# Attention schedule: extra products at other steps, small products behind the scores, statistics ahead of the maximum, a stage one step later

## The chip, the cores and the metric

One core of a Trainium2 chip runs the whole program in one launch. The metric is the device time in microseconds of one execution. The engines are TensorE (PE; PEld is its weight load), VectorE (DVE), ScalarE (ACT), GpSimd (POOL) and SyncE (SP), which issues most DMAs. Each takes its instructions in order, and they signal each other by semaphores.

## The reference, cut to what matters

The model adds to x, one after the other: a gated feed-forward net, a state space block, the feed-forward net again, a mixture of experts, an attention, and the mixture again. Only the attention is touched. It has 2 sequences of 1024 tokens and 16 heads of 64, so 32 heads of 1024 x 1024 scores:

```python
dots = jnp.einsum('bhid,bhjd->bhij', q, k) * SCALE
m = jax.nn.softmax(dots, axis=-1)
diag = jnp.diagonal(m, axis1=-2, axis2=-1)
mu = diag.mean(axis=-1, keepdims=True)
sd = diag.std(axis=-1, ddof=1, keepdims=True)
keep = jnp.abs((diag - mu) / sd) <= Z_THRESH
valid = keep[..., :, None] & keep[..., None, :]
masked = jnp.where(valid, dots, NEG)
attn = jax.nn.softmax(masked, axis=-1)
...
out = jnp.einsum('bhij,bhjd->bhid', attn, v)
```

A head thus needs its whole score matrix once for the softmax's diagonal, then a mask out of the diagonal's statistics, the largest unmasked score of each row, and the scores again for the masked softmax.

## The kernel before

**Steps.** The attention is a software pipeline. A head's rows are cut into 8 blocks of 128 (`BLK`), and one step t handles one block of each stage. `due(t, offset, n)` (L1576) gives the head h and block k for which t = offset + 8h + k, with k < n. So an offset modulo 8 is the place of a stage in the period of eight steps in which each head goes through. The offsets stand at L1572 and L1573. Every engine has its own loop over t (`attention_pe`, `_act`, `_dve`, `_pool`, `_sp`) and in it a fixed order of `if`s, which is the order of its queue.

**Stages of a head.** QK projection (one step, `AT_QK`): ScalarE rounds it to a high part (`round_qk`, L2142), VectorE forms the low part (`rest_of_qk`, L2237), and SyncE copies both with the halves of the partitions swapped into `at_kq` (`move_parts`, four DMAs, L1805 and L1806). Scores (8 steps, L1957 and L1958): VectorE takes the diagonal (L2253), ScalarE the exponential with its sum (L2157). Statistics: reciprocals (`first_stats`), the mean by a small product (L1965, `negate_mean` reads it), deviations on ScalarE, the sum of squares by a second small product, `keeps` (L2287 to L2295, ending in `at_dropped`), and the mask turned into a row by a third (L1972, `mask_rows`), which SyncE spreads through DRAM. Best (8 steps, L1997 and L1998): scores again in high parts, masked and reduced to `at_row_max` by VectorE (L2262). A fourth small product turns the maxima (L1972, `shift_rows`), and two DMAs bring them to `at_shift_row`. Turned scores (8 steps, L2007 and L2008, and the shift product at L1878, with `at_shift_row` as an operand): ScalarE's exponential (`at_e`, L2165), VectorE's cast to a high part (L2382), GpSimd's subtraction for the low part (L2409). Two steps later `weigh` multiplies by the values (L1878 into `at_pv_ps`). ScalarE copies the sum of a head (L2204); the denominators go by DMA to VectorE (L2343, L2345), back through DRAM and spread (L1838), and GpSimd normalizes (L2421). For every second head there is an output projection, and VectorE adds it to x (L2364). Values are projected in two parts for every four heads (`group_due`, L1927).

**PSUM.** All these products but `weigh` share three tiles, `at_ps0` to `at_ps2`, in turn. `attention_slots` (L1604) lists the slots in order: in each step turned scores, scores, a slot that a small product and the best product of the step share (the small one first, in its corners), and then an extra one (QK, values or output) where one is due. `slot_free` (L1640) makes a product wait for the reader of the slot three before it:

```python
    kind, h, k = m.slot_order[n - 3][-1]
```

and a best product also for the reader of the small one in its slot.

**Order on TensorE within a step** (L2087 on): turned scores, small product, scores, weighing, best product, extra, weighing, extra. Where weighing and best are both due, products run as pairs on the upper and lower half of the rows, and the extra is in two halves around the second weighing.

**Before and behind.** A normalization of x stands ahead of the first step; the last head has its own end without DMAs (`last_norm`, L2315).

Of the kernel before, what the change touches and what calls it, by code (L numbers as in the profile page):

```python
# [9 lines left out]
ALU = mybir.AluOpType  # L10
# [10 lines left out]
BIG = 2.0 ** 100  # L21
# [23 lines left out]
BLK = SEQ // P  # L45
NH = BATCH * HEADS
# [1513 lines left out]

AT_FIRST, AT_LAST = -BLK * 2, BLK * (NH - 1) + BLK * 5 + 1
STATS, DEVS = 8, 5
HI, LO = 0, 1
TOP, LOW = slice(0, HD), slice(HD, P)
# [2 lines left out]
PARTS = 4  # L1569


AT_SPLIT, AT_QK, AT_SCORES, AT_STATS, AT_MEAN, AT_SQUARE, AT_MASK, AT_BEST, AT_SHIFT = -11, -8, 0, 8, 9, 10, 11, 13, 21  # L1572
AT_TURNED, AT_PV, AT_PV_OUT, AT_RECIP, AT_SPREAD, AT_NORM, AT_OUT = 22, 24, 32, 34, 35, 37, 39  # L1573


def due(t, offset, n=1):  # L1576
# [12 lines left out]


def pair_due(t):
    at = due(t, AT_OUT)
    return at[0] if at and at[0] % 2 == 1 else None


def small_due(t):
# [262 lines left out]
def attention_pe(c, m):  # L1859
# [227 lines left out]
    for t in range(AT_FIRST, AT_LAST):  # L2087
        weighed, tested = due(t, AT_PV, BLK), due(t, AT_BEST, BLK)
        apart = bool(weighed and tested)
        if at := due(t, AT_TURNED, BLK):  # L2090
            turned_scores(*at)
        if at := due(t, AT_MEAN):
            mean(at[0])
        if at := due(t, AT_SQUARE):
# [2 lines left out]
            turn_mask(at[0])  # L2097
        if at := due(t, AT_SHIFT):
            turn_shift(at[0])
        if at := due(t, AT_SCORES, BLK):  # L2100
            scores(*at)
        if apart:
            weigh(*weighed, False)
        if tested:
# [119 lines left out]
def attention_dve(c, m):  # L2224
# [107 lines left out]
    for t in range(AT_FIRST, AT_LAST):  # L2332
# [3 lines left out]
                attention_later_norm_dve(c, m)  # L2336
        if at := group_due(t - 1):
            rest_of_values(*at)
        if (at := due(t, AT_RECIP)) and at[0] == LAST:
            last_norm()  # L2340
        elif at:
            dve.wait_ge(sem["den_move"], 16 * (at[0] + 1))
            dve.eng.tensor_scalar(m.den[:], m.den[:], 1.0 / BIG, None, ALU.max).then_inc(sem["at_recip"])  # L2343
            dve.wait_ge(sem["at_recip"], 2 * at[0] + 1)
            dve.eng.reciprocal(m.recip[:], m.den[:]).then_inc(sem["at_recip"])  # L2345
        if (h := pair_due(t - 1)) is not None:
            pair, b = h % HEADS // 2, h // HEADS
            cols = slice(b * SEQ, (b + 1) * SEQ)
            dve.wait_ge(sem["at_out"], h // 2 + 1)
            dve.wait_ge(sem["attn_load"], 2 * 16)  # L2350
            dve.wait_ge(sem["attn_out_load"], 16)
            if h == LAST:
                for hf in range(2):
                    cols = slice(b * SEQ + hf * CH, b * SEQ + (hf + 1) * CH)
                    dve.wait_ge(sem["at_out"], h // 2 + hf + 1)
                    dve.wait_ge(sem["x_attn"], h // 2)
                    dve.eng.tensor_tensor(c.x[:, cols], c.x[:, cols], slot("out", h)[:, HALF[hf]],
                                          ALU.add).then_inc(sem["x_attn"])
            elif pair == 0:
                dve.eng.scalar_tensor_tensor(c.x[:, cols], slot("out", h)[:], c.b_out[:, 0:1], c.x[:, cols],  # L2360
                                             ALU.add, ALU.add).then_inc(sem["x_attn"])
            else:
                dve.wait_ge(sem["x_attn"], h // 2)
                dve.eng.tensor_tensor(c.x[:, cols], c.x[:, cols], slot("out", h)[:], ALU.add).then_inc(sem["x_attn"])  # L2364
        if at := due(t, AT_MEAN):
            negate_mean(at[0])
        if at := due(t, AT_SQUARE):
            negate_square(at[0])
        if at := due(t, AT_MASK):
            mask_rows(at[0])  # L2370
        if at := due(t, AT_SHIFT):
            shift_rows(at[0])
        if at := due(t, AT_SCORES, BLK):
            diagonal(*at)
        if at := due(t, AT_STATS):
            first_stats(at[0])
        if at := due(t, AT_TURNED, BLK):
            e = at[0] * BLK + at[1]
            dve.wait_ge(sem["at_exp"], e + 1)
# [2 lines left out]
            dve.eng.tensor_copy(m.e_hi[e % 3][:], m.e[e % 2][:]).then_inc(sem["at_hi"])  # L2382
        if at := due(t, AT_BEST, BLK):
            best(*at)
        if at := due(t, AT_SQUARE):
            keeps(at[0])
    dve.wait_ge(sem["x_attn"], ATTN_SUMS)


# [269 lines left out]
```

## Time and profile before

| | |
|---|---|
| median of 3 runs | 1979.87 us (1979.25 to 1979.98) |
| the profiled execution | 1980.71 us, span from first to last instruction 1979.4 us, clock 0.987 |
| PE busy | 1786.4 us, 90% |
| DVE busy | 1404.6 us, 71% |
| POOL busy | 1193.8 us, 60% |
| ACT busy | 1159.7 us, 59% |
| at_e_lo, POOL L2409 | 613.1 us, 256 times 2395 ns |
| maximum, DVE L2262 | 314.1 us, 256 times 1227 ns |
| cast at_e_hi, DVE L2382 | 247.8 us, 256 times 968 ns |

Busy times of engines run beside each other. A matmul's record overlaps the next one's, so lengths of steps are read from starts of the same kind of product, not from sums of durations. "[idle before <-releaser]" on a row is the time for which the engine did nothing ahead of it, and what ended that. The attention runs from about 712 us to 1854 us of the span.

### The profile page before, as it was taken

The page shows a single profiled execution, that of the slowest core. Times are in us where ns is not written, and L with a number is a line of the kernel's source. Part 1 is how long each engine was busy: PE and PEld are TensorE (multiplying, and loading weights), DVE is VectorE, ACT ScalarE, POOL GpSimd, SP SyncE. Part 2 cuts the span into 40 slices and gives each one's busy share as a digit, 9 for nine tenths or more (in the row PEclk, how much of TensorE's full clock was granted, in tenths as well). Part 3 has the DMA queues.
Part 4 walks back from the last instruction along what each step waited for, and adds up shares of the span by engine and source line. Part 5 has one row for each costly group of instructions (what it writes and reads, how often), then busy time and mean ns, then how long its engine had stood idle before and what let it go on. Part 6 is the DMA issues. An engine that isn't in the chain of part 4 may idle for free. (4 is left out here: it accounts for less than half of the span.)

```text
span 1979.4 us, 29905 instructions
## 1 busy us (share of the span) xinstructions
PE 1786.4 (90%) x11064; PEld 1213.2 (61%) x11064; DVE 1404.6 (71%) x2493; ACT 1159.7 (59%) x1715; POOL 1193.8 (60%) x660
## 2 busy tenths in 40 slices
PE   9998999789998986899989899898989898988888
PEld 5873444336875654666666667666666676665466
DVE  5617899986427754677777777777777777787676
ACT  5326777745326456666666666666666666663544
POOL 5542767963535430576666767676767666667454
PEclk9998999999999997999999999999999999999999
DMA  2000000000000013212122121212121212100100
GB/s 96 1 0 0 0 0 0 0 1 0 1 20 29 1 51 75 52 45 58 45 48 55 38 64 35 68 35 58 45 57 46 57 45 56 44 12 17 53 6 16
DMA packets 43665, 66.03 MB, mean 33 GB/s; under 512 B 24769, under 2 KB 26177, under 8 KB 43265
## 3 DMA queue, kind: packets, MB, share of 16 engines
q1 hardware_dynamic: 43056, 63.54, 12.4%
q8 instruction: 88, 1.44, 0.3%
q10 hardware_dynamic: 432, 0.59, 0.1%
q14 instruction: 57, 0.46, 0.1%
q0 software_dynamic: 32, 0.00, 0.0%
HBM read 29.05 MB, written 1.24 MB: 15 GB/s over the span
## 5 line engine op out<-in xcount | busy, mean ns | idle before, releaser
L2409 POOL TENSOR_TENSOR at_e_lo<-at_e,at_e_hi 128x1024 fp32r<-128x1024 f32 x256 | 613.1, 2395 | 353.9 <-DVE at_e_hi L2382 348.4
L2165 ACT ACTIVATE at_e<-at_ps,at_dropped 128x1024 f32<-128x1024 f32 x256 | 285.7, 1116 | 199.7 <-PE at_ps L1878 189.3
L2157 ACT ACTIVATE at_ps<-at_ps,at_neg_diag 128x1024 f32<-128x1024 f32 x256 | 278.6, 1089 | 138.3 <-DVE at_neg_diag L2253 137.0
L2262 DVE CUSTOM_DVE_ANT_0 at_ps<-at_ps,at_mask 128x1024 f32<-128x1024 f32 x256 | 314.1, 1227 | 3.0 <-PE at_ps L1998 1.3
L2382 DVE CAST at_e_hi<-at_e 128x1024 fp32r<-128x1024 f32 x256 | 247.8, 968 | 31.8 <-ACT at_e L2165 30.1
L1957 PE MATMUL at_ps<-at_kq,at_qk 64*128 64x512 f32 x768 | 235.3, 414 | 6.9 <-DVE at_row_max L2262 4.5
L1958 PE MATMUL at_ps<-at_qk,at_kq 64*128 64x512 f32 x768 | 235.7, 414 | 0.0
L2007 PE MATMUL at_ps<-at_qk,at_kq 64*128 64x512 f32 x768 | 224.4, 398 | 1.6 <-DVE at_row_max L2262 1.2
L2008 PE MATMUL at_ps<-at_kq,at_qk 64*128 64x512 f32 x768 | 224.6, 399 | 0.0
L1878 PE MATMUL at_pv_ps<-at_e_hi,at_v_hi 64*128 64x512 f32 x980 | 218.0, 436 | 0.0
L1056 POOL TENSOR_TENSOR mb_work<-mb_work,mb_c 128x1024 f32<-128x1024 f32 x64 | 151.6, 2370 | 97.7 <-DVE mb_work L1025 97.6
L421 POOL TENSOR_TENSOR ffn_lo<-ffn_hid,ffn_hi 128x512 fp32r<-128x512 f32 x96 | 127.2, 1328 | 132.1 <-DVE ffn_hi L338 132.1
L1878 PE MATMUL at_pv_ps<-at_e_hi,at_v_lo 64*64 64x512 f32 x980 | 195.3, 390 | 0.0
L1878 PE MATMUL at_pv_ps<-at_e_lo,at_v_hi 64*128 64x512 f32 x980 | 194.6, 389 | 0.0
L2253 DVE CUSTOM_DVE_ANT_0 at_junk_diag<-at_ps,ident 128x128 bf16<-128x128 f32 x256 | 74.0, 290 | 154.9 <-PE at_ps L1958 154.2
L2007 PEld LDWEIGHTS at_ps<-at_qk,at_kq 64*128 64x128 f32 x768 | 139.8, 185 | 34.4 <-DVE at_row_max L2262 4.2
L1957 PEld LDWEIGHTS at_ps<-at_kq,at_qk 64*128 64x128 f32 x768 | 134.2, 190 | 34.3 <-issue 10.2
L1025 DVE TENSOR_TENSOR_SCAN mb_work<-mb_work,mb_u_ps 128x1024 f32<-128x1024 f32 x64 | 146.3, 2286 | 6.4 <-PE mb_y_ps L652 1.2
L1500 POOL TENSOR_TENSOR moe_hid_lo<-moe_prod,moe_hid_hi 128x512 fp32r<-128x512 f32 (+1 forms) x72 | 92.8, 1290 | 95.6 <-ACT moe_hid_hi L1332 95.6
L338 DVE CAST ffn_hi<-ffn_hid 128x512 fp32r<-128x512 f32 x96 | 64.0, 671 | 120.8 <-ACT ffn_hid L309 119.5
L2008 PEld LDWEIGHTS at_ps<-at_kq,at_qk 64*128 64x128 f32 x768 | 139.8, 185 | 6.3 <-issue 4.2
L652 PE MATMUL mb_y_ps<-mb_work,ident 128*128 128x512 f32 x256 | 132.1, 602 | 8.4 <-DVE mb_dtx L949 6.8
(392 smaller groups left out, 4243.1 us busy)
## 6 DMA issues: line engine op xcount, KB each, us to landing
at_kq<-at_qk SPq DMA_DIRECT2D x128, 256.0 KB, 4.2
at_mask<-at_mask_dram SPq DMA_DIRECT2D x32, 256.0 KB, 3.6
at_recips<-at_recip_row SPq DMA_DIRECT2D x31, 256.0 KB, 4.4
ffn_h_raw<-in_h SPq DMA_DIRECT2D x2, 1024.0 KB, 8.0
at_head_w_raw<-in_w_qkv SPq DMA_DIRECT2D x32, 64.0 KB, 3.9
x<-in_x SPq DMA_DIRECT2D x4, 256.0 KB, 5.0
moe_gate_in<-in_gate_in SPq DMA_DIRECT2D x2, 512.0 KB, 4.0
moe_up_in<-in_up_in SPq DMA_DIRECT2D x2, 512.0 KB, 4.3
```

What stands on the lines that cost most here:

```text
L1025: dve.eng.tensor_tensor_scan(m.state[i % MB_STATES_HELD], m.d_a[i % MB_DECAYS], m.u_ps[:], 0.0, ALU.mult, ALU.add).then_inc(sem["mb_scan"])
L1056: pool.eng.tensor_tensor(m.state[i % MB_STATES_HELD], m.state[i % MB_STATES_HELD], m.c_sb[i % 3], ALU.mult).then_inc(sem["mb_hc"])
L1878: mm = pe.eng.matmul(bank, w[rows], moving[rows], start=first, stop=last)
L1957: pe.eng.matmul(ps[:, HALF[0]], own[TOP, q, rows], swapped[TOP, k, HALF[0]], start=(n == 0), stop=(n == 2))
L1958: mm = pe.eng.matmul(ps[:, HALF[1]], swapped[LOW, q, rows], own[LOW, k, HALF[1]], start=(n == 0), stop=(n == 2))
L2007: pe.eng.matmul(ps[:, HALF[0]], swapped[TOP, k, keys], own[TOP, q, HALF[0]], start=(n == 0), stop=False)
L2008: pe.eng.matmul(ps[:, HALF[1]], own[LOW, k, keys], swapped[LOW, q, HALF[1]], start=(n == 0), stop=False)
L2157: act.eng.activation(ps[:], ps[:], ACT.Exp, scale=SCALE, bias=m.small["neg_diag"][s][:, blk:blk + 1], accum_out=m.small["sums"][s][:, blk: ...
L2165: act.eng.activation(m.e[e % 2][:], slot("turned_scores", h, blk)[:], ACT.Exp, scale=SCALE, bias=m.small["dropped"][h % SLOTS][:, blk:blk ...
L2262: dve.eng.tensor_tensor_reduce(out=ps[:], in0=ps[:], in1=m.mask[h % 2][:], scale=1.0, scalar=-BIG, op0=ALU.add, op1=ALU.max, accum_out=m.s ...
L2382: dve.eng.tensor_copy(m.e_hi[e % 3][:], m.e[e % 2][:]).then_inc(sem["at_hi"])
L2409: pool.eng.tensor_tensor(m.e_lo[e % 3][:], m.e[e % 2][:], m.e_hi[e % 3][:].bitcast(F32), ALU.subtract).then_inc(sem["at_lo"])
```

## The change

The offsets move: the head weights' split from -11 to -6, QK from -8 to -3; turned scores from 22 to 23, and all that follows them by one step (weighing, its copy, reciprocal, spread, normalization); the output projection from 39 to 43, for the last head 40. Values follow the weighing (`group_due`), so they move by one step too. On TensorE the scores go ahead of the small products. On VectorE the diagonal and `first_stats` go ahead of the small products' readers, `keeps` ahead of the cast and the maximum, and the denominator's two operations behind the small readers. No instruction is added or removed but for the loops' one more step.

```diff
--- before.py
+++ after.py
@@ -1560,7 +1560,7 @@
 
 
 
-AT_FIRST, AT_LAST = -BLK * 2, BLK * (NH - 1) + BLK * 5 + 1
+AT_FIRST, AT_LAST = -BLK * 2, BLK * (NH - 1) + BLK * 5 + 2
 STATS, DEVS = 8, 5
 HI, LO = 0, 1
 TOP, LOW = slice(0, HD), slice(HD, P)
@@ -1569,8 +1569,8 @@
 PARTS = 4
 
 
-AT_SPLIT, AT_QK, AT_SCORES, AT_STATS, AT_MEAN, AT_SQUARE, AT_MASK, AT_BEST, AT_SHIFT = -11, -8, 0, 8, 9, 10, 11, 13, 21
-AT_TURNED, AT_PV, AT_PV_OUT, AT_RECIP, AT_SPREAD, AT_NORM, AT_OUT = 22, 24, 32, 34, 35, 37, 39
+AT_SPLIT, AT_QK, AT_SCORES, AT_STATS, AT_MEAN, AT_SQUARE, AT_MASK, AT_BEST, AT_SHIFT = -6, -3, 0, 8, 9, 10, 11, 13, 21
+AT_TURNED, AT_PV, AT_PV_OUT, AT_RECIP, AT_SPREAD, AT_NORM, AT_OUT, AT_LAST_OUT = 23, 25, 33, 35, 36, 38, 43, 40
 
 
 def due(t, offset, n=1):
@@ -1589,8 +1589,10 @@
 
 
 def pair_due(t):
+    if t == LAST * BLK + AT_LAST_OUT:
+        return LAST
     at = due(t, AT_OUT)
-    return at[0] if at and at[0] % 2 == 1 else None
+    return at[0] if at and at[0] % 2 == 1 and at[0] != LAST else None
 
 
 def small_due(t):
@@ -2089,6 +2091,8 @@
         apart = bool(weighed and tested)
         if at := due(t, AT_TURNED, BLK):
             turned_scores(*at)
+        if at := due(t, AT_SCORES, BLK):
+            scores(*at)
         if at := due(t, AT_MEAN):
             mean(at[0])
         if at := due(t, AT_SQUARE):
@@ -2097,8 +2101,6 @@
             turn_mask(at[0])
         if at := due(t, AT_SHIFT):
             turn_shift(at[0])
-        if at := due(t, AT_SCORES, BLK):
-            scores(*at)
         if apart:
             weigh(*weighed, False)
         if tested:
@@ -2336,13 +2338,6 @@
                 attention_later_norm_dve(c, m)
         if at := group_due(t - 1):
             rest_of_values(*at)
-        if (at := due(t, AT_RECIP)) and at[0] == LAST:
-            last_norm()
-        elif at:
-            dve.wait_ge(sem["den_move"], 16 * (at[0] + 1))
-            dve.eng.tensor_scalar(m.den[:], m.den[:], 1.0 / BIG, None, ALU.max).then_inc(sem["at_recip"])
-            dve.wait_ge(sem["at_recip"], 2 * at[0] + 1)
-            dve.eng.reciprocal(m.recip[:], m.den[:]).then_inc(sem["at_recip"])
         if (h := pair_due(t - 1)) is not None:
             pair, b = h % HEADS // 2, h // HEADS
             cols = slice(b * SEQ, (b + 1) * SEQ)
@@ -2362,18 +2357,26 @@
             else:
                 dve.wait_ge(sem["x_attn"], h // 2)
                 dve.eng.tensor_tensor(c.x[:, cols], c.x[:, cols], slot("out", h)[:], ALU.add).then_inc(sem["x_attn"])
+        if at := due(t, AT_SCORES, BLK):
+            diagonal(*at)
+        if at := due(t, AT_STATS):
+            first_stats(at[0])
         if at := due(t, AT_MEAN):
             negate_mean(at[0])
         if at := due(t, AT_SQUARE):
             negate_square(at[0])
+            keeps(at[0])
         if at := due(t, AT_MASK):
             mask_rows(at[0])
         if at := due(t, AT_SHIFT):
             shift_rows(at[0])
-        if at := due(t, AT_SCORES, BLK):
-            diagonal(*at)
-        if at := due(t, AT_STATS):
-            first_stats(at[0])
+        if (at := due(t, AT_RECIP)) and at[0] == LAST:
+            last_norm()
+        elif at:
+            dve.wait_ge(sem["den_move"], 16 * (at[0] + 1))
+            dve.eng.tensor_scalar(m.den[:], m.den[:], 1.0 / BIG, None, ALU.max).then_inc(sem["at_recip"])
+            dve.wait_ge(sem["at_recip"], 2 * at[0] + 1)
+            dve.eng.reciprocal(m.recip[:], m.den[:]).then_inc(sem["at_recip"])
         if at := due(t, AT_TURNED, BLK):
             e = at[0] * BLK + at[1]
             dve.wait_ge(sem["at_exp"], e + 1)
@@ -2382,8 +2385,6 @@
             dve.eng.tensor_copy(m.e_hi[e % 3][:], m.e[e % 2][:]).then_inc(sem["at_hi"])
         if at := due(t, AT_BEST, BLK):
             best(*at)
-        if at := due(t, AT_SQUARE):
-            keeps(at[0])
     dve.wait_ge(sem["x_attn"], ATTN_SUMS)
 
 
```

## Rows read from the trace of the kernel before

**Rows 1.** PE, PEld, DVE, ACT, POOL: busy us (instructions); clock, DMA share, GB/s

```profile
795.00:1735.00 940.00, 852.92 (x7270) 624.70 (x7266) 703.34 (x1510) 609.57 (x910) 640.81 (x305) 1.00 0.20 50
```

**Rows 2.** Waits of PE: line, what ended them, total us, times, longest

```profile
PE at_ps L1965 <- DVE at_qk L2237: 43.7, 28, 1.6
PE at_ps L1972 <- DVE at_dropped L2295: 26.3, 23, 2.1
```

**Rows 3.** Timeline, PE (start us, us): marks opening steps 2, 3, 4, 6, 0, 1, 2

```profile
973.65 0.40 PE L1878 MATMUL at_ps<-at_shift_row,at_minus 64*128 64x512 f32 x2
...
977.20 0.39 PE L1878 MATMUL at_ps<-at_shift_row,at_minus 64*128 64x512 f32 x2
...
981.88 0.39 PE L1878 MATMUL at_ps<-at_shift_row,at_minus 64*128 64x512 f32 x2
...
988.63 0.39 PE L1878 MATMUL at_ps<-at_shift_row,at_minus 64*128 64x512 f32 x2
...
995.23 0.39 PE L1878 MATMUL at_ps<-at_shift_row,at_minus 64*128 64x512 f32 x2
...
1000.61 0.39 PE L1878 MATMUL at_ps<-at_shift_row,at_minus 64*128 64x512 f32 x2
...
1005.89 0.39 PE L1878 MATMUL at_ps<-at_shift_row,at_minus 64*128 64x512 f32 x2
```

**Rows 4.** Timeline, PE: marks around values and QK; around an output projection

```profile
1054.97 0.39 PE L1878 MATMUL at_ps<-at_shift_row,at_minus 64*128 64x512 f32 x2
...
1059.62 0.40 PE L1878 MATMUL at_ps<-at_shift_row,at_minus 64*128 64x512 f32 x2
...
1063.19 0.39 PE L1878 MATMUL at_ps<-at_shift_row,at_minus 64*128 64x512 f32 x2
...
1067.77 0.41 PE L1878 MATMUL at_ps<-at_shift_row,at_minus 64*128 64x512 f32 x2
...
1227.59 0.41 PE L1878 MATMUL at_ps<-at_shift_row,at_minus 64*128 64x512 f32 x2
...
1232.54 0.41 PE L1878 MATMUL at_ps<-at_shift_row,at_minus 64*128 64x512 f32 x2
```

**Rows 5.** Timeline, PE: the mean's product of heads 8 and 24

```profile
1002.57 0.27 PE L1965 MATMUL at_ps<-at_row_sum_parts,at_ones 64*128 64x2 f32 x2 [1.57 <-DVE at_qk L2237]
...
1540.93 0.27 PE L1965 MATMUL at_ps<-at_row_sum_parts,at_ones 64*128 64x2 f32 x2 [1.56 <-DVE at_qk L2237]
```

**Rows 6.** Timeline, DVE: casts, a maximum, the low part of QK

```profile
990.21 0.69 DVE L2382 CAST at_e_hi<-at_e 128x1024 fp32r<-128x1024 f32 x1 [0.16 <-ACT at_e L2165]
...
993.52 2.75 DVE L2382 CAST at_e_hi<-at_e 128x1024 fp32r<-128x1024 f32 x1 [0.17 <-ACT at_e L2165]
...
996.20 1.22 DVE L2262 CUSTOM_DVE_ANT_0 at_ps<-at_ps,at_mask 128x1024 f32<-128x1024 f32 x1
...
1001.20 1.23 DVE L2237 TENSOR_TENSOR at_qk<-at_ps,at_qk 128x1024 fp32r<-128x1024 f32 x1 [0.72 <-ACT at_qk L2142]
...
1061.54 1.08 DVE L2382 CAST at_e_hi<-at_e 128x1024 fp32r<-128x1024 f32 x1
```

**Rows 7.** Timeline, POOL: low parts and a normalization

```profile
987.73 2.40 POOL L2409 TENSOR_TENSOR at_e_lo<-at_e,at_e_hi 128x1024 fp32r<-128x1024 f32 x1
...
990.26 2.90 POOL L2421 TENSOR_TENSOR at_heads_out<-at_pv_sb,at_recips 64x1024 f32<-64x1024 f32 x1
...
993.33 2.40 POOL L2409 TENSOR_TENSOR at_e_lo<-at_e,at_e_hi 128x1024 fp32r<-128x1024 f32 x1 [0.17 <-POOL at_heads_out L2421]
...
996.35 2.38 POOL L2409 TENSOR_TENSOR at_e_lo<-at_e,at_e_hi 128x1024 fp32r<-128x1024 f32 x1 [0.63 <-DVE at_e_hi L2382]
```

**Rows 8.** One tile's instructions, ns min/median/max, first and last start

```profile
L2292 DVE TENSOR_SCALAR at_keep<-at_dev,at_limit,at_varies x32: 290/1033/1072, 758.0 to 1779.4; 128x8 f32<-128x8 f32 x32
```

**Rows 9.** SyncE's last of four part transfers, and L1806's times to landing

```profile
1003.07 1.03 SPq L1806 DMA_DIRECT2D at_kq<-at_qk  x1
...
DMA to landing us min/median/max: 3.8/4.5/6.0
```

## The prediction

> **What bounds the kernel now.** I read three views in turn. First, the busy time of each engine in the steady stretch of the attention: TensorE is busy 852.92 of 940 us at a granted clock of 1.00, and VectorE, GpSimd and ScalarE 703, 641 and 610 us [rows 1]. So TensorE's work sets the pace, and about 9% of it is waiting. Second, TensorE's waits: the product for the mean (L1965) waits 28 times for VectorE to read the QK projection (L2237), 43.7 us, and the turned mask (L1972) waits 23 times for `at_dropped`, 26.3 us [rows 2]. Third, the timeline, with the shift product (L1878 on `at_shift_row`) as the mark that occurs once a step. The difference of two marks is the length of a step, and that, not the idle time shown, is the price of a wait: after a wait the pipeline also has to fill again.
>
> The marks give a price list. Two steps without an extra or a small product take 6.60 us (988.63 to 995.23) [rows 3], so one takes 3.30. The step with the square takes 3.55 and the one with the turned shift 6.75 - 3.30 = 3.45, so a small product that waits for nothing costs 0.25 or 0.15 [rows 3]. The mask's step takes 4.68, 1.23 over its unstalled 3.45. The mean's step takes 5.28, 1.73 over the square's. A QK projection that waits for nothing takes its step to 4.58, so costs 1.28 [rows 4]; in the head of rows 3 that step took 5.38, 0.80 more. A values product costs 4.65 - 3.30 = 1.35, and the step after it, which waits for its reader, takes 3.57, 0.27 over [rows 4]. An output projection costs 4.95 - 3.30 = 1.65 [rows 4].
>
> Per head the work alone comes to 8 x 3.30 + 1.28 (QK) + 0.80 (four small products) + 0.68 (two values parts in four heads) + 0.83 (one output in two heads) = 29.99 us. Sixteen heads took 538.36 us, 33.65 each [rows 5]. So **3.66 us per head are waits**.
>
> **The change part by part.** A step's products go turned scores, small, scores, weighing, best, extra; after the change the small one comes behind the scores. An extra takes one of three PSUM tiles in turn, so what stands three slots behind it needs its reader. In the kernel before, that is the small product in the next step where there is one, and TensorE is held with scores, weighing and best queued behind it. By residue of the step in its head of eight, small products stand at 1, 2, 3 and 5 in both kernels. Extras move from QK at 0, values at 6 and 2, output at 7 to QK at 5, values at 7 and 3, output at 3; each is then followed by 6, 0 or 4, where nothing small stands.
>
> 1. *Mean.* 1.73 us per head goes. QK's reader is now due only at the best product of step 6. It ends 1.82 us behind the mark (1001.20 + 1.23 - 1000.61), and the product waiting for it began at 1.96 [rows 3, 6, 5]. The same arrangement exists already behind the values at step 6, and cost 0.27 [rows 4]. I take 0.27 back; bounds 0 and 0.4.
>
> 2. *Mask.* `keeps` runs ahead of the high-part cast and the maximum, and the mask's product behind the scores, so `at_dropped` is there more than a microsecond early, and the values' reader is gone from this step. 1.23 us goes. In exchange four tiny VectorE operations, and the two of the denominator, stand ahead of the cast. `at_keep` takes 0.29 us when nothing is in its way and 1.03 at the median [rows 8]: the difference is waiting for GpSimd. Ahead of the cast the sum is some 0.8 us on VectorE; the product that would wait for it (the mask, then the best) has about that much room. On TensorE I take 0, bounds 0 and 0.4 per head.
>
> 3. *QK at 0.* Its step holds 0.80 us of waiting in the head of rows 3, which is the late maximum behind the slow cast of point 5, and less where an output or values step goes before. It goes from here, and comes back as point 5.
>
> 4. *QK's parts by DMA.* The projection is now three steps ahead of its scores instead of eight. The last of the four transfers is issued 2.46 us behind the mark (1003.07 - 1000.61) and lands 4.5 us later at the median, 6.0 at most [rows 3, 9]: 6.96 to 8.46. Two steps are then 3.57 + 3.30 = 6.87, and the scores stand 0.23 behind that mark (estimate), at 7.1. So TensorE may wait 0 to 1.4 us. Taken at 0, because point 5's wait comes later in the same stretch and covers it. Uncovered, it costs up to 1.4 per head.
>
> 5. *GpSimd's normalization.* It moves from step 5 to 6, behind the subtraction `at_e_lo`, and the head weights' split from 5 to 2. I follow it from step 6's mark (0). The cast behind a PSUM reader starts at 1.92 (1061.54 - 1059.62) and takes 0.69 alone [rows 4, 6]. `at_e_lo` follows at 2.69 for 2.40, the normalization 0.13 behind it at 5.22 [rows 7]. The next cast stands 1.58 behind its mark (990.21 - 988.63), at 3.57 + 1.58 = 5.15: just ahead. The normalization takes 2.90, to 8.12, the next `at_e_lo` starts at 8.29 (gap 0.17) and ends at 10.69 [rows 7]. The cast of step 0 is due at 6.87 + 1.58 = 8.45, so it is late by 0.16 and is held, as the one at 993.52 is, which took 2.75 us and was 0.54 behind GpSimd's end [rows 6, 7]. The maximum then ends 1.69 behind GpSimd's end, at 12.38 [rows 6, 7]. In the kernel before such a delay met the QK step's best product. Now the mean at step 1 needs that PSUM tile: it would be ready 0.92 behind its mark (estimate), 6.87 + 3.30 + 0.92 = 11.1, and waits until about 12.5. **1.4 us come back** in the three heads of four that have no values product at step 7 (that one gives 1.35 of room): 1.05 per head.
>
> The Trainium skill, page "SBUF — State Buffer", section "SBUF: two separate sides", says that VectorE's fast modes and GpSimd share a port pair by an exclusive lock, held for a whole instruction. By that rule the cast at 993.52 is held by `at_e_lo`, and the trace agrees: 2.75 us for work of 0.69. The rule speaks against moving `keeps` ahead of the cast.
>
> 6. *Values and output.* Their readers are waited for at steps 4 and 0 by the best product: 0.27 twice in four heads, 0.14 per head. The output's reader (one addition) has the room. The work itself is unchanged.
>
> Sum per head: -3.66 + 0.27 + 1.05 + 0.14 = -2.20 us, a period of about 31.45. Over the 28 heads in which everything runs, -61.6. Everything after the scores is **one step later**, so the drain has one more step, bound by the loop cast, subtraction, cast: 3.02 us from start to start [rows 7]: +3.0. The filling stretch has the QK parts due after three short steps, but smaller waits for statistics; I take 0, bounds -4 and +6. The total is -58.6. The profiled execution took 1980.71 us for a span of 1979.4; that is 0.8 us over the median of 1979.87, so the sum goes on the median: **1921 us**.
>
> **The rivals.** (a) *The normalization costs nothing.* If the cast of step 0 comes 0.16 us earlier or `at_e_lo` later, point 5 vanishes: 1921 - 28 x 1.05 = 1892 us. For it: a margin smaller than the jitter of a DMA. Against it: the casts and GpSimd repeat to 0.1 us, and in the kernel before the same race is lost by 0.19 (993.33 against 993.52) [rows 6, 7]. (b) *The queue of VectorE and GpSimd binds more.* After the held cast the two recover only 3.30 - 3.02 = 0.28 us a step [rows 3, 7], and `keeps`, the split at step 2 and the denominator's operations eat that. If the mask's and the shift's products then also wait, with the QK parts uncovered, 0.4 to 1.0 us per head come on top: 1932 to 1949, middle 1941. (c) *Slower than before: QK's parts.* SyncE is one queue; the parts stand behind the spread of the reciprocals (step 4, which waits for a write that itself waits for VectorE's step 3) and the shift (step 5). Up to 1.4 us past the scores' time is covered; from there each microsecond is 28 us. It decides above 1.4 + 2.1 = 3.5 us past, a landing 8.1 us after the last issue instead of 4.5 to 6.0 [rows 9]; at 9.1 the time is about 2007. Nothing in rows 9 comes near. (d) *The change doesn't do what it says:* the small products still share a slot with the best product and wait for the maximum before it for as long as they waited for QK. Then nothing moves but the drain: 1980 to 1983. The room of 0.7 us in an undisturbed step speaks against it.
>
> If the lock goes to the normalization in the tie at 5.15 against 5.22, the held cast is step 7's, and the waits are about 0.9 at step 0's best product and 0.4 at the mean: 1.3 in place of 1.4, the same forecast. The skill's rule (the first to start gets the port pair) would give the time of my forecast.
>
> **How the numbers follow.** Forecast 55%, range 1908 to 1934 by the bounds of points 1, 2 and the filling; (a) 20%; (b) 19%; (c) 3%; (d) 3%. The range reaches to (a) and the end of (b): 1890 to 1950. Within 0.2% (4 us) is what a measurement can't tell from no change. Faster 0.94, same 0.03, slower 0.03.
>
> **What would show it.** After: TensorE's wait for L2237 at the mean gone, and a small one at the best product (L1997-L1998) in its place; the wait for `at_dropped` gone; the step with QK 4.75 (1.28 + 3.45) long; the mean's step either 3.55, which is (a), or near 4.9 with a wait for `at_row_max`, which is the forecast; scores waiting for `at_kq` by DMA at most 1.4 us. I am wrong if TensorE still waits more than 2.5 us per head, or if the marks of plain steps move from 3.30.

## The result and the profile after

The changed kernel takes **1923.93 us** (median, 1923.52 to 1926.94) against 1979.92 in the same comparison: a ratio of 0.9726, 95% interval 0.9714 to 0.9737. 1921 was forecast. The profiled execution took 1923.52 us for a span of 1922.0 us.

First TensorE's busy time and its waits. Ahead of the windows row stand the columns of [rows 1]; the waits are ordered as in [rows 2]. Lines have shifted by two: L1967 is the mean's product, L1959 and L1960 are the scores, L1880 takes the place of L1878.

```profile
795.00:1675.00 880.00, 854.66 (x7234) 631.25 (x7232) 650.25 (x1508) 596.71 (x908) 629.32 (x306) 1.00 0.22 54
```

```profile
PE at_ps L1967 <- DVE at_row_max L2264: 16.2, 18, 1.2
...
PE at_ps L1959 <- DMA at_kq<-at_qk: 14.2, 10, 6.4
```

TensorE is busy 97% of the stretch, where it was 91% [rows 1]. Both waits of [rows 2] are gone: nothing at the mean waits for QK's reader, nothing at the mask for `at_dropped`. Two new ones stand in their place, and both were named ahead: the mean's product waits for the maximum, and the first scores of a head wait for the QK parts by DMA. The second line is mostly the filling stretch: three of its ten waits are there, with 10.3 of the 14.2 us.

The marks of a head without values or output, on the timeline of TensorE. They open steps 5, 6, 7, 0, 1, 2 and 3:

```profile
968.40 0.39 PE L1880 MATMUL at_ps<-at_shift_row,at_minus 64*128 64x512 f32 x2
...
973.16 0.39 PE L1880 MATMUL at_ps<-at_shift_row,at_minus 64*128 64x512 f32 x2
...
976.74 0.40 PE L1880 MATMUL at_ps<-at_shift_row,at_minus 64*128 64x512 f32 x2
...
980.04 0.39 PE L1880 MATMUL at_ps<-at_shift_row,at_minus 64*128 64x512 f32 x2
...
983.83 0.39 PE L1880 MATMUL at_ps<-at_shift_row,at_minus 64*128 64x512 f32 x2
...
988.35 0.40 PE L1880 MATMUL at_ps<-at_shift_row,at_minus 64*128 64x512 f32 x2
...
991.77 0.40 PE L1880 MATMUL at_ps<-at_shift_row,at_minus 64*128 64x512 f32 x2
```

Steps 5, 6, 7, 0, 1 and 2 take 4.76, 3.58, 3.30, 3.79, 4.52 and 3.42 us. Set beside [rows 3], a plain step is still 3.30; QK's step is 4.76 where it was 5.38; the mean's is 4.52 where it was 5.28, for another reason. Two rows of the mean's product, 16 heads apart as in [rows 5], give 506.58 / 16 = 31.66 us a head instead of 33.65:

```profile
985.72 0.27 PE L1967 MATMUL at_ps<-at_row_sum_parts,at_ones 64*128 64x2 f32 x2 [0.82 <-DVE at_row_max L2264]
...
1492.30 0.27 PE L1967 MATMUL at_ps<-at_row_sum_parts,at_ones 64*128 64x2 f32 x2 [1.03 <-DVE at_row_max L2264]
```

Where the mean's wait comes from is on the timelines of GpSimd and VectorE in the same head, the counterparts of [rows 6] and [rows 7]:

```profile
978.38 2.87 POOL L2422 TENSOR_TENSOR at_heads_out<-at_pv_sb,at_recips 64x1024 f32<-64x1024 f32 x1
981.42 2.40 POOL L2410 TENSOR_TENSOR at_e_lo<-at_e,at_e_hi 128x1024 fp32r<-128x1024 f32 x1 [0.17 <-POOL at_heads_out L2422]
```

```profile
978.33 0.70 DVE L2385 CAST at_e_hi<-at_e 128x1024 fp32r<-128x1024 f32 x1 [0.17 <-ACT at_e L2167]
...
982.16 2.21 DVE L2385 CAST at_e_hi<-at_e 128x1024 fp32r<-128x1024 f32 x1
984.30 1.22 DVE L2264 CUSTOM_DVE_ANT_0 at_ps<-at_ps,at_mask 128x1024 f32<-128x1024 f32 x1
```

The normalization starts 5.22 us behind step 6's mark (973.16), with the cast of step 7 just ahead of it by 0.05. The low part of step 7 holds GpSimd from 981.42 to 983.82, and the cast of step 0 is held with it: 2.21 us for 0.69 of work. Its maximum ends at 985.52, and the mean's product, due about 0.92 behind 983.83, starts at 985.72.

**The whole difference.** By the marks of steps 24 and 248 of both traces the period is 33.60 us before and 31.56 after, 28 x 2.04 = 57.2 us. From the first scores to the mark of step 24 it is 59.1 and 59.7. Behind the mark of step 248 it is 2.0 us more, the added step. What lies ahead of the first scores was 2.7 us shorter in this execution (733.8 against 736.5 us). The forecast had no term for that, and it isn't shown to come from the change: the runs below with QK at its old step have 734.1 to 735.5 us there. Together -57.3, and the spans differ by 57.4.

### The profile page after: what moved, and what is told of

It reads as the page before. It is cut to its first block and busy times, and to the rows that moved or that the text cites. A ratio compares the mean times of both kernels' runs of the same rounds, so it can differ in the third digit from the quotient of the medians.

```text
span 1922.0 us, 29893 instructions
## 1 busy us (share of the span) xinstructions
PE 1792.2 (93%) x11058; PEld 1222.8 (64%) x11058; DVE 1349.5 (70%) x2493; ACT 1148.6 (60%) x1715; POOL 1187.4 (62%) x660
## 3 DMA queue, kind: packets, MB, share of 16 engines
q1 hardware_dynamic: 43056, 63.54, 12.8%
## 5 line engine op out<-in xcount | busy, mean ns | idle before, releaser
L2159 ACT ACTIVATE at_ps<-at_ps,at_neg_diag 128x1024 f32<-128x1024 f32 x256 | 278.5, 1088 | 60.3 <-DVE at_neg_diag L2255 60.1
L2385 DVE CAST at_e_hi<-at_e 128x1024 fp32r<-128x1024 f32 x256 | 237.3, 927 | 33.2 <-ACT at_e L2167 32.8
L1959 PE MATMUL at_ps<-at_kq,at_qk 64*128 64x512 f32 x768 | 226.3, 403 | 17.0 <-DMA at_kq<-at_qk 14.2
L1960 PE MATMUL at_ps<-at_qk,at_kq 64*128 64x512 f32 x768 | 226.5, 403 | 0.0
L2009 PE MATMUL at_ps<-at_qk,at_kq 64*128 64x512 f32 x768 | 224.4, 398 | 1.8 <-DVE at_qk L2239 1.2
L1880 PE MATMUL at_pv_ps<-at_e_hi,at_v_hi 64*128 64x512 f32 x976 | 224.9, 451 | 0.8 <-issue 0.8
L2010 PE MATMUL at_ps<-at_kq,at_qk 64*128 64x512 f32 x768 | 224.3, 398 | 0.0
L1880 PE MATMUL at_pv_ps<-at_e_lo,at_v_hi 64*128 64x512 f32 x976 | 195.8, 389 | 0.9 <-POOL at_e_lo L2410 0.9
L1880 PE MATMUL at_pv_ps<-at_e_hi,at_v_lo 64*64 64x512 f32 x976 | 196.3, 391 | 0.0
L1959 PEld LDWEIGHTS at_ps<-at_kq,at_qk 64*128 64x128 f32 x768 | 142.8, 190 | 56.6 <-DMA at_kq<-at_qk 25.1
L2009 PEld LDWEIGHTS at_ps<-at_qk,at_kq 64*128 64x128 f32 x768 | 139.8, 185 | 38.8 <-issue 7.9
L1960 PEld LDWEIGHTS at_ps<-at_qk,at_kq 64*128 64x128 f32 x768 | 142.7, 190 | 1.6
L2010 PEld LDWEIGHTS at_ps<-at_kq,at_qk 64*128 64x128 f32 x768 | 139.8, 185 | 2.1 <-issue 0.5
```

The source lines that it names most:

```text
L1880: mm = pe.eng.matmul(bank, w[rows], moving[rows], start=first, stop=last)
L1959: pe.eng.matmul(ps[:, HALF[0]], own[TOP, q, rows], swapped[TOP, k, HALF[0]], start=(n == 0), stop=(n == 2))
L1960: mm = pe.eng.matmul(ps[:, HALF[1]], swapped[LOW, q, rows], own[LOW, k, HALF[1]], start=(n == 0), stop=(n == 2))
L2009: pe.eng.matmul(ps[:, HALF[0]], swapped[TOP, k, keys], own[TOP, q, HALF[0]], start=(n == 0), stop=False)
L2010: pe.eng.matmul(ps[:, HALF[1]], own[LOW, k, keys], swapped[LOW, q, HALF[1]], start=(n == 0), stop=False)
L2159: act.eng.activation(ps[:], ps[:], ACT.Exp, scale=SCALE, bias=m.small["neg_diag"][s][:, blk:blk + 1], accum_out=m.small["sums"][s][:, blk: ...
```

## Experiments

All edits but the first two runs' are against the changed kernel. The period is always (mark of step 248 - mark of step 24) / 28; the fill is from the first scores to the mark of step 24. Period and fill are of the profiled execution, which for "QK at 0" (1910.8) and "small first" (1982.3) was the fastest, 5 us under the median. The ratios are to the kernel before as it ran beside each run: its medians there were 1983.0, 1978.3 and 1979.5 us, so a difference of two medians in this table can be off by a few us.

| run | median us | ratio to before, 95% | period us | fill us |
|---|---|---|---|---|
| before | 1979.9 | | 33.60 | 59.1 |
| changed | 1923.9 | 0.9714 to 0.9737 | 31.56 | 59.7 |
| offsets alone | 2000.5 | 1.0073 to 1.0107 | 33.65 | 71.9 |
| order alone | 1943.4 | 0.9784 to 0.9817 | 32.46 | 56.8 |
| keeps last | 1948.9 | 0.9819 to 0.9851 | 32.32 | 62.1 |
| small first | 1987.1 | 1.0033 to 1.0064 | 33.12 | 72.8 |
| QK at 0 | 1915.9 | 0.9671 to 0.9703 | 31.34 | 51.9 |
| normalization at 5 | 1900.4 | 0.9570 to 0.9602 | 30.73 | 59.7 |
| normalization on 64 columns | 1893.2 | 0.9554 to 0.9586 | 30.74 | 59.3 |
| QK at 0, normalization at 5 | 1930.6 | 0.9733 to 0.9765 | 32.01 | 54.3 |
| norm. at 5, one transfer by ScalarE | 1900.6 | 0.9586 to 0.9618 | 30.58 | 60.1 |
| norm. at 5, early QK | 1893.0 | 0.9554 to 0.9585 | 30.74 | 51.9 |
| the same and one transfer by ScalarE | 1889.2 | 0.9533 to 0.9565 | 30.61 | 53.7 |

### The two halves of the change

**Offsets alone.** The kernel before with the diff's hunks on the offsets and `pair_due`, none of those on order.

> The kernel before with the new offsets alone (QK at residue 5, values at 7 and 3, output at 3, one step later), the old order on TensorE and VectorE. My theory: the QK reader's wait at the mean goes (1.73 us a head), but the late maximum of step 0 now holds the mean's product, which stands ahead of the scores at 0.23 behind the mark and so waits about 2.1 us in three heads of four, and the mask's wait for at_dropped (1.23) stays. Period about 33.5 us instead of 33.6: 1972 to 1982 us, about 1976, so nearly no gain. Rival (the extras' steps are where the gain comes from): 1.73 + 0.5 - 0.41 us a head for 28 heads, about 1930 us.

2000.49 us, slower than before by 0.7 to 1.1%. TensorE's waits in this run:

```profile
PE at_ps L1974 <- DVE at_dropped L2297: 41.6, 31, 2.4
PE at_ps L1967 <- DVE at_row_max L2264: 33.1, 28, 1.8
```

The period was foreseen (33.5, measured 33.65): the extras' new steps take QK's reader away from the mean, and the late maximum takes its place almost in full, since the small product still stands ahead of the scores. The 24 us over my expectation lie mostly outside: the fill is 12.8 us longer than before, and the stretch behind the mark of step 248 is 7.7 us longer, where the change's is 2.0. The fill I had in no sum. The rival is out.

**Order alone.** The kernel before with the hunks on order.

> The kernel before with the new order alone (scores ahead of the small product, diagonal and first statistics ahead, keeps ahead of cast and maximum), the old offsets, so QK still stands in the step before the mean. My theory: the mean's product is due 0.92 instead of 0.23 behind the mark and waits about 1.0 instead of 1.7 for QK's reader; the mask's wait goes but for the head in four with a values product before it (1.0 left). About 2.1 us a head, no added step at the end: 1915 to 1930 us, about 1921, as much as the whole change. Rival (the order only brings the mask's wait, 1.23 us a head): about 1945 us.

1943.37 us: the rival's number (1945), not mine (1921), though not for the rival's reason. Its waits name what I had left out:

```profile
PE at_ps L1965 <- DVE at_qk L2237: 24.7, 28, 0.9
PE at_ps L1878 <- DMA at_shift_row<-at_shift_rows: 15.8, 31, 1.5
```

The mean's wait for QK's reader falls from 1.6 to 0.9 us each, as foreseen: its step is 4.60. But the turned shift, now behind the scores, brings its row 0.7 us later, and the shift product of step 6 waits for the DMA 31 times: step 5 averages 4.10 us where it was 3.47. With turned scores at 23 that wait is gone but for single ones of at most 0.6 us. So "one step later" seems to earn its place here; it was not run by itself. The nearest pair is this run and "QK at 0" below, which differ by the stages one step later (the normalization too) and by the steps of values and output: periods of 32.46 and 31.34 us, and step 5 has 0.65 of the difference.

So the order alone brings a gain and the offsets alone cost; together they bring 56 us, where their separate effects (1983.0 - 1943.4 = 39.6 and 1983.0 - 2000.5 = -17.5, against the kernel before as it ran beside them) add up to 22.

**Keeps last.**

```diff
             negate_square(at[0])
-            keeps(at[0])
...
         if at := due(t, AT_BEST, BLK):
             best(*at)
+        if at := due(t, AT_SQUARE):
+            keeps(at[0])
```

> The changed kernel with keeps back behind the maximum in its step, all else as changed. My theory: at_dropped then comes about 2.1 us behind step 3's mark and the mask's product is due at 0.92, so it waits about 1.2 us in every head: about 1957 us (1945 to 1962). Rival (putting the small products behind the scores already gives them the time, and keeps only delays the cast): 1924 us or a little less, 1918 to 1926.

1948.9 us: 25 us lost, where I said 33. The wait for `at_dropped` is back, and it is the only one that grew by more than a microsecond:

```profile
PE at_ps L1974 <- DVE at_dropped L2297: 24.7, 31, 2.3
```

Step 3 goes from 3.64 to 4.42 us in a head without extra there: 0.8 instead of the 1.2 that I took. The fill is 2.4 us longer.

**Small first.** On TensorE `scores(*at)` again behind the four small products.

> The changed kernel with the small products ahead of the scores again on TensorE, all else as changed. My theory: the mean waits 0.7 us longer for the late maximum in three heads of four, the two statistics products cost 0.25 instead of 0.12, the mask's operand is ready anyway, and the filling stretch gets some 5 us longer as in the run of the offsets alone: about 1950 us (1940 to 1958). Rival (with the extras moved, the order on TensorE no longer matters): 1924 to 1930 us.

1987.11 us, 37 us over my expectation, with executions from 1982 to 1995. Both reasons were underrated. TensorE's waits, and VectorE's maximum of step 2 beside the mark and the mask's product of step 3:

```profile
PE at_ps L1967 <- DVE at_row_max L2264: 33.3, 28, 1.8
PE at_ps L1974 <- DVE at_row_max L2264: 20.5, 32, 1.8
```

```profile
1015.11 1.23 DVE L2264 CUSTOM_DVE_ANT_0 at_ps<-at_ps,at_mask 128x1024 f32<-128x1024 f32 x1
```

```profile
1015.55 0.39 PE L1880 MATMUL at_ps<-at_shift_row,at_minus 64*128 64x512 f32 x2
...
1016.53 0.22 PE L1974 MATMUL at_ps<-ident,at_dropped 64*8 64x64 f32 x2 [0.60 <-DVE at_row_max L2264]
```

The maximum ends at 1016.34, 0.79 behind the mark, because `keeps` now stands ahead of it. A small product ahead of the scores is due at 0.23 and waits for it; behind the scores, at 0.92, it doesn't. So `keeps` ahead of the maximum pays only with the small products behind the scores. The fill is 13 us longer than the changed kernel's: with the new offsets, the order of TensorE is worth that much there. Part of it is a slower clock, as the section on the fill shows.

### The held cast

**Normalization at step 5.** One number: `AT_NORM` 38 to 37.

```diff
-... AT_NORM, AT_OUT, AT_LAST_OUT = 23, 25, 33, 35, 36, 38, 43, 40
+... AT_NORM, AT_OUT, AT_LAST_OUT = 23, 25, 33, 35, 36, 37, 43, 40
```

> The changed kernel with GpSimd's normalization one step earlier (offset 37, residue 5, as in the kernel before) and nothing else. My theory of point 5: the held cast is then step 6's, whose step follows the long QK step, VectorE and GpSimd have caught up by the mean, and the mean's product waits for nothing in all heads: its step falls from 4.7 to about 3.5 us in three heads of four; scores still wait some 0.3 us for the QK parts. About 1895 us (1890 to 1905). Rival (the loop of VectorE and GpSimd is simply full, wherever the normalization stands): the wait comes at another small product, 1918 to 1930 us.

1900.4 us: 23.5 us better than the change. The marks of steps 0, 1 and 2:

```profile
977.59 0.39 PE L1880 MATMUL at_ps<-at_shift_row,at_minus 64*128 64x512 f32 x2
...
981.40 0.39 PE L1880 MATMUL at_ps<-at_shift_row,at_minus 64*128 64x512 f32 x2
...
984.81 0.39 PE L1880 MATMUL at_ps<-at_shift_row,at_minus 64*128 64x512 f32 x2
```

The mean's step is 3.41 instead of 4.52; the period falls by 0.83. Step 0 keeps its 3.81: that wait for the QK parts isn't covered now. It averages 0.40 above a plain step, where I had taken 0.3, so it accounts for some three of the five us over my 1895. Held casts have not gone: they are those of steps 6 and 7 now, of 1.15 and 0.94 us at the median, where the change holds those of steps 0 and 1, of 2.28 and 1.26. Hardly a product waits for what follows them there.

**Normalization on 64 columns.** It stays at step 6, and does 64 of the 1024 columns; the rest of the heads' output is left at a constant.

```diff
+    pool.eng.memset(m.heads_out[:], 1.0).then_inc(sem["at_spare"])
+    pool.wait_ge(sem["at_spare"], 6)
...
-pool.eng.tensor_tensor(m.heads_out[place, :], m.pv_sb[0:HD, :], m.recips[:],
+pool.eng.tensor_tensor(m.heads_out[place, 0:HD], m.pv_sb[0:HD, 0:HD], m.recips[:, 0:HD],
```

> The changed kernel, its normalization still at step 6, but done on 64 of 1024 columns only (the rest of the heads' output is left at a constant, so that part of the computation is left out). If the held cast comes from GpSimd's 2.9 us of normalization, the mean's wait for at_row_max goes and the time is that of the run with the normalization at step 5, 1895 to 1902 us. If that run's gain came from something else than the collision (another order of the queues): 1915 to 1924 us.

1893.2 us, just under the range, with a period of 30.74, the same as with the whole normalization at step 5. So its 2.9 us of GpSimd are the whole cause of the mean's wait, and at step 5 they cost nothing in the period. The spans of the two runs differ by 7.8 us, 6.5 of it behind the mark of step 248 (236.9 against 243.4 us); why there, no run parts.

### What QK's move is worth

**QK at 0.** `AT_QK` and `AT_SPLIT` back at -8 and -11, all else as changed.

> The changed kernel with QK and the head weights' split back at their old offsets (-8 and -11, residues 0 and 5), all else as changed. It isolates the move of QK's step. My theory from the run of the order alone: the mean then waits for QK's reader again (about 1.2 us in its step, in every head), but that takes the place of the late maximum's wait (0.86 a head in the changed kernel), and the wait behind step 5 (0.29) and for the QK parts (0.4 at step 0) go. So QK's move alone is worth next to nothing as long as the normalization stands at step 6: 1922 us (1913 to 1932). Rival (moving the extras away from small products is what pays): 1.2 to 1.7 us a head more, 1955 to 1970 us.

1915.9 us (1910.8 to 1918.8): faster than the whole change, and by the intervals clearly so. The marks of steps 0, 1 and 2:

```profile
972.69 0.39 PE L1880 MATMUL at_ps<-at_shift_row,at_minus 64*128 64x512 f32 x2
...
977.29 0.40 PE L1880 MATMUL at_ps<-at_shift_row,at_minus 64*128 64x512 f32 x2
...
982.10 0.40 PE L1880 MATMUL at_ps<-at_shift_row,at_minus 64*128 64x512 f32 x2
```

The mean's step takes 4.81, with QK's reader and the late maximum in it. The change has 4.52 there, 3.79 in step 0 (here 4.60 with QK, so 3.32 without it) and 0.28 more behind step 5. That is 0.5 more in this head; over 28 heads the late maximum is absent in one of four, and the two periods differ by 0.22. And the fill, 51.9 us, is 7.8 shorter. The period says that QK's move gains nothing, the fill that it costs.

**QK at 0, normalization at 5.** The fourth corner.

> The run with QK back at residue 0, and the normalization at step 5 as well: the fourth corner of QK's step against the normalization's. If QK's move only pays once the late maximum no longer stands at the mean (my theory now), this one stays at a period of about 31.2 us against 30.73 with QK at 5, the mean waiting 1.2 us for QK's reader in every head, but has the short filling stretch: 1908 us (1903 to 1914), slower than 1900. Rival (QK's move is worth nothing in either case): 1893 to 1900 us.

1930.6 us, 22 us over what I expected and slower than with the normalization at 6. On VectorE a cast and the maximum behind it, on TensorE step 0's best product:

```profile
977.16 2.74 DVE L2385 CAST at_e_hi<-at_e 128x1024 fp32r<-128x1024 f32 x1 [0.16 <-ACT at_e L2167]
979.82 1.22 DVE L2264 CUSTOM_DVE_ANT_0 at_ps<-at_ps,at_mask 128x1024 f32<-128x1024 f32 x1
```

```profile
981.15 0.50 PE L1999 MATMUL at_ps<-at_kq,at_qk 64*128 64x512 f32 x1 [0.47 <-DVE at_row_max L2264]
```

Without QK between steps 5 and 6 nothing seems to give VectorE and GpSimd time: step 7's cast is held, as in [rows 6], step 0's best product waits (that step is 5.35), and a step later the mean waits for QK's reader all the same. The two waits stand in different steps and add up; with the normalization at 6 they fell together. The four periods:

| | normalization at 6 | at 5 |
|---|---|---|
| QK at residue 0 | 31.34 | 32.01 |
| QK at residue 5 | 31.56 | 30.73 |

QK's move is worth 1.28 us a head with the normalization at 5, and -0.22 with it at 6. The second is nothing within the spread: the profiled execution behind 31.34 was 5 us, or 0.18 a head, under its median.

### The QK parts and the fill

**One transfer by ScalarE's queue.**

```diff
-            sp.eng.dma_start(swapped[TOP, part, :].bitcast(F32), own[LOW, part, :].bitcast(F32)).then_inc(done, 16)
+            if part == HI:
+                sp.eng.dma_start(swapped[TOP, part, :].bitcast(F32), own[LOW, part, :].bitcast(F32)).then_inc(done, 16)
...
+        if at := due(t, AT_QK + 1):
+            act.wait_ge(sem["at_qk_lo"], at[0] + 1)
+            act.eng.dma_start(m.kq[at[0] % SLOTS][TOP, LO, :].bitcast(F32), m.qk[at[0] % SLOTS][LOW, LO, :].bitcast(F32)
+                              ).then_inc(sem[f"parts_move{at[0] % 2}"], 16)
```

> The run with the normalization at step 5, and the last of the four QK part transfers issued by ScalarE's queue, right behind its exponential, instead of as SyncE's fourth. My theory: the last issue comes 0.6 us earlier, and the scores' wait of 0.3 to 1.2 us for the parts at step 0 goes, while ScalarE has the room: about 1892 us (1888 to 1896). Rival (the transfers themselves are the limit, or ScalarE's issue delays the sums): 1899 to 1906 us.

1900.6 us, unchanged and in the rival's range, though the period fell from 30.73 to 30.58 (4 us in all). For head 0 ScalarE's queue stands behind the later heads' normalization, so the first scores came 3.8 us later (739.2 against 735.4). Averaged over the heads, step 0 fell from 3.70 us to 3.54, which is 0.16 of the 0.40 us that it stood above 3.30. The rest of its wait stayed, and the trace says why: the transfer was issued 0.6 us earlier, as planned (1.84 behind the mark instead of 2.46), but took 5.3 us to land at the median instead of 4.8, so that it landed only 0.1 earlier. The queue was not the limit; the transfers were, which is the rival's first half.

**Early QK.** QK, split and transfers 5 steps earlier for heads 0 to 3 only, in the kernel with the normalization at 5.

```diff
+EARLY = 4
...
+def head_due(t, offset):
...
+    if (at := due(t, offset - 5)) and at[0] < EARLY:
+        return at
+    return at if (at := due(t, offset)) and at[0] >= EARLY else None
...
-        if at := due(t, AT_QK):
+        if at := head_due(t, AT_QK):
```

> The run with the normalization at step 5, and QK (with its split and DMAs) at the old offset for heads 0 to 3, whose projections fall in the filling stretch, at the new one from head 4 on. In the traces so far the stretch from the first scores to the mark of step 24 takes 59.7 us with QK at -3 and 51.9 with QK at -8. My theory (in the filling stretch three short steps don't cover the QK parts' transfers): 7 to 8 us less, about 1893 us (1890 to 1896), the period unchanged at 30.7. Rival (the filling stretch is bound by the statistics' chain, and the 7.8 us came from elsewhere): 1898 to 1902 us.

1893.0 us: as expected, with a fill of 51.9 us. The period stayed at 30.74, so the 7.8 us are the QK parts in the fill. In the changed kernel TensorE waits there for them twice at length (scores of heads 1 and 2), and behind both its granted clock is 0.50, half of full speed (750 to 754 us, and the row of 770 to 780):

```profile
749.65 0.79 PE L1959 MATMUL at_ps<-at_kq,at_qk 64*128 64x512 f32 x1 [6.43 <-DMA at_kq<-at_qk]
...
769.98 0.79 PE L1959 MATMUL at_ps<-at_kq,at_qk 64*128 64x512 f32 x1 [3.35 <-DMA at_kq<-at_qk]
```

```profile
770.00:780.00 10.00, 8.45 (x38) 5.67 (x40) 6.23 (x23) 5.48 (x13) 0.00 (x0) 0.50 0.00 0
```

So the fills differ by waits and by the clock that follows them. The granted clock over the fill is 0.80 before and after the change, 0.87 with QK at 0 and with early QK, 0.69 and 0.70 with the offsets alone and small first. For nearly the same products TensorE is busy 42.0, 41.9, 39.7, 39.7, 44.7 and 45.6 us. From these busy times I estimate that some 2.2 of the 7.8 us are the slower clock, and some 3.7 of the 13 of small first.

**Both, head 0 by SyncE.**

> The run with the early projections, and ScalarE's queue for the fourth part transfer from head 1 on (head 0 by SyncE, since ScalarE's queue is behind the later normalization there and cost 3.4 us before the first scores). The transfer itself gave 0.15 us a head in the trace: about 1889 us (1886 to 1893). Rival (ScalarE's issue costs in the filling stretch what it gives later): the same as the run without it.

**1889.2 us** (1887.9 to 1890.4), the fastest, as expected, 0.9549 of before (0.9533 to 0.9565), 35 us below the change. Its fill is 1.8 us longer than without ScalarE's transfer (53.7), so the rival is half right; the period gives 3.6 back.

## Why the prediction was right, point by point

**The steps, averaged over the 28 heads.** The forecast's terms laid out by step, and the marks:

| step | 0 | 1 | 2 | 3 | 4 | 5 | 6 | 7 | sum |
|---|---|---|---|---|---|---|---|---|---|
| forecast | 3.37 | 4.60 | 3.55 | 4.61 | 3.37 | 4.73 | 3.57 | 3.64 | 31.44 |
| measured | 3.71 | 4.28 | 3.42 | 4.75 | 3.40 | 4.76 | 3.59 | 3.64 | 31.56 |

The forecast of 1921 was 3 us off. Its terms gave -58.6 us and came to -54.6 in the profiled executions, nearly all of the gap in the period (61.6 forecast, 57.2 measured). The 2.7 us ahead of the first scores, in no term, made up for over half of that. This part of the hit is luck.

**What bounds it, and the price list:** right. A plain step stayed at 3.30. The floor of 29.99 us is still 0.6 below the fastest period.

**Point 1, mean:** right. QK's reader costs 0.28 in step 6 (0.27 taken). What the runs add: it wasn't the move of QK that earned this, since with QK back at 0 the period is no longer. The order's half of it, from 1.6 to 0.9 us of waiting, needs no move.

**Point 2, mask:** right in its main term, off by a small one. The mask waits for nothing, and `keeps` took less than I feared, as its row, the counterpart of [rows 8], shows:

```profile
L2294 DVE TENSOR_SCALAR at_keep<-at_dev,at_limit,at_varies x32: 289/444/919, 756.2 to 1715.0; 128x8 f32<-128x8 f32 x32
```

The step with the mask took 3.64 instead of 3.45, inside my bounds. The statistics' small products cost 0.12 behind the scores instead of the 0.25 that I carried over. The 0.26 of the two nearly cancels the 0.19 of the mask.

**Points 3 and 5, the late maximum:** right to 0.1 us along the whole chain of one head, from step 6's mark: normalization 5.22 (5.22 forecast), next low part 8.26 (8.29), maximum's end 12.36 (12.38), the mean's product 12.56 (12.5). With the run on 64 columns the cause is shown, not only argued. Per head it costs 0.83 (31.56 against 30.73) instead of 1.05, because part of it stands in the same stretch as the wait for the QK parts.

**Point 4, QK's parts:** half right. The last transfer was issued 2.46 behind the mark. The line's times to landing are near those of [rows 9], 0.2 over at the most:

```profile
DMA to landing us min/median/max: 3.8/4.6/6.2
```

But I misread them: this line issues the second and the fourth transfer, and 4.5 is the median of both. The trace before has 3.85 for the second and 4.81 for the fourth. So the last part lands at 7.28, not 6.96, behind the mark, and behind the 7.1 at which the scores are due. Accordingly the scores waited 0.2 in most heads, for 0.3 of step length, and 0.4 on average. I had it covered by the mean's wait. That holds: steps 0 and 1 together take 8.31 us in the head above, and in the heads where step 0 takes 4.4 to 4.5, step 1 takes only 3.8, 8.3 together. On average steps 0 and 1 take 7.99 where the forecast's terms give 7.97. With the normalization at 5 the cover is gone, and the 0.3 to 1.2 us count.

**Point 6:** right (3.60 in a step 4 behind values).

**The fill, taken at 0:** the net was right (59.1 and 59.7), the reason wasn't seen. It is effects that cancel: QK's parts due after three short steps cost 7.8 us (QK at 0: 51.9), clock included, and the rest of the change gives 7.2 back. Most of that is the new order meeting the new offsets, since without it they need 71.9; the order alone gives 2.3. In the forecast this was one bound of -4 to +6. Behind the mark of step 248, with the added step in it, it came to 2.0 us for 3.0.

**The range:** 1908 to 1934 doesn't follow from the bounds named for it. Added up, 28 heads of points 1 and 2 and the filling stretch give 1910 to 1942. The measured time lies in both.

**Rivals.** (a), the normalization costing nothing, is the kernel with it one step earlier, by 1892 forecast and 1900 measured. (b) didn't come in the change, but is what the small-first run shows: `keeps` eats VectorE's room, and the mask's product waits for the maximum. (c) was never near. (d), no effect, is close to what happens if the order of TensorE alone is left out: 1987.

What I got wrong is in the expectations. I priced each half by its steady period and left out the fill and the drain (12.8 and 7.7 us in the offsets' run) or took the fill too low (13 for 5 in small first). I also left out the DMA behind the turned shift (order alone), and, at the fourth corner, that two waits which fall into one step count once and in two steps twice.

What stays open: why the transfers of some heads (late by 0.8 us in three heads in a row) land later, why the drain of the offsets' run is so long, what the later turned scores and the moves of values and output are worth each by itself, and which of VectorE's reorderings matters in the fill.

## What to carry to other kernels

Price a moved step from the marks of one repeated instruction, with and without each neighbour, and then follow the engine that shares something with the mover (here GpSimd with VectorE) through the next three steps: the chain came out to 0.1 us. After a gain of this kind test each moved offset by itself in its new surroundings, since one of them (QK's) was worth nothing and became worth 1.28 us a head when another was moved by one step. Treat filling and draining stretches as stages with their own schedule: the same offset that is free in steady state cost 8 us there, and a different one for the first four heads took it back.

## What the runs showed of the hardware

- A cast of VectorE from SBUF to SBUF (0.69 us alone) ends 0.54 to 0.57 us behind GpSimd's instruction that was running when it came, if that is a low part (casts of 2.74 and 2.21 us above) or a normalization (30 casts in the run with it at step 5, a median of 1.15 us). Shrinking GpSimd's normalization to 64 columns took the number of held casts from 73 to 26 and the mean's wait away: this agrees with the exclusive port pair that the Trainium skill's page "SBUF — State Buffer", section "SBUF: two separate sides", describes.
- The other way round GpSimd's normalization takes 2.87 to 2.90 us when a cast starts 0.05 ahead of it, and 2.37 to 2.41 in other heads.
- Four transfers of 256 KB inside SBUF, issued one behind the other, land 3.15, 3.85, 4.30 and 4.81 us after their issues at the median (changed kernel). Issued 0.6 us earlier by another queue, the last took 5.3 us and landed only 0.1 us earlier.
- TensorE's granted clock in the fill: 1.00 at its start, 0.50 (the lower level, 1.2 GHz) from 750 to 754 and from 770 to 780 us, behind waits of 6.43 and 3.35 us, and 1.00 again from 790. Scores' products, 0.23 us apart at 1.00, start 0.43 apart at 0.50.
